# Broadcasts in attention: two chained transfers of 64 partitions instead of one of 128

## What is computed

```python
def _forward(hidden_states, wq, wk, wv, conv_q_w, conv_k_w, conv_v_w, A_log, dt_bias, ...):
    x = hidden_states
    q = short_conv(x @ wq, conv_q_w).reshape(B, T, H, DK)      # H, DK, DV = 16, 128, 128
    k = short_conv(x @ wk, conv_k_w).reshape(B, T, H, DK)
    v = short_conv(x @ wv, conv_v_w).reshape(B, T, H, DV)
    ...                                                        # feats: entropy, errors of k @ proxy_w against v
    hf = silu(silu(feats @ mlp_w1 + mlp_b1) @ mlp_w2 + mlp_b2)
    beta_fast = jax.nn.sigmoid(beta_base + beta_delta)         # and slow; lam, amp_fast, amp_slow likewise, from hf
    ...
    decay_fast = jnp.exp(g_chan[None, None] * amp_fast[..., None])
    decay_slow = jnp.exp(g_chan[None, None] * amp_slow[..., None])
    o_fast = delta_rule(qs, k_unit, v, beta_fast, decay_fast)
    o_slow = delta_rule(qs, k_unit, v, beta_slow, decay_slow)
    o = lam[..., None] * o_fast + (1.0 - lam[..., None]) * o_slow
    ...
    return o.reshape(B, T, H * DV) @ wo

def delta_rule(q, k, v, beta, decay):
    def step(S, inp):
        qt, kt, vt, bt, gt = inp
        Sd = S * gt[..., None]
        v_pred = jnp.einsum('bhk,bhkv->bhv', kt, Sd)
        S_new = Sd + jnp.einsum('bhk,bhv->bhkv', kt * bt[..., None], vt - v_pred)
        ot = jnp.einsum('bhk,bhkv->bhv', qt, S_new)
        return (S_new, ot)
```

## Time and profile before

| | us |
|---|---|
| median of 3 runs | 4295.09 |
| lowest, highest | 4289.88, 4296.61 |
| the profiled execution's own time | 4301.73 |
| its span, first to last instruction | 4299.9 |
| TensorE busy (share of the span) | 4000.7 (93%) |
| VectorE busy | 3105.3 (72%) |
| ScalarE busy | 2296.8 (53%) |
| GpSimd busy | 933.6 (22%) |
| share of 16 DMA engines in the queue of SyncE's transfers | 20.2% |

### The profile page before, as it was taken

The page is one execution under the profiler, slowest core; times in us unless marked ns, Lnnn a source line. Parts: engine busy times, 40 slices in busy tenths (PEclk is TensorE's granted clock), DMA queues, the critical chain, the costliest instruction groups (busy, mean ns, idle before and its releaser), DMA issues. The chain is left out here.

```text
span 4299.9 us, 179869 instructions
## 1 busy us (share of the span) xinstructions
PE 4000.7 (93%) x76866; PEld 2486.6 (58%) x76866; DVE 3105.3 (72%) x5135; ACT 2296.8 (53%) x6321; POOL 933.6 (22%) x1927
## 2 busy tenths in 40 slices
PE   7999999999999999999999999757879789999998
PEld 4667767767676676767667676522333334444443
DVE  4788888888888888888888887478999991212221
ACT  4577776676676667676676766444344331111110
POOL 1333333333333333333233333100000000000000
PEclk8999999999999999999999999778989899999999
DMA  2222222222221212212122221142323332000000
GB/s 76 65 60 71 65 69 68 58 76 66 63 68 59 77 52 75 70 56 78 57 70 70 63 71 49 41 148 72 94 83 96 92 121 89 29 1 30 0 20 10
DMA packets 133721, 277.31 MB, mean 64 GB/s; under 512 B 21004, under 2 KB 62496, under 8 KB 129472
## 3 DMA queue, kind: packets, MB, share of 16 engines
q1 hardware_dynamic: 132784, 265.60, 20.2%
q10 hardware_dynamic: 144, 0.20, 0.0%
HBM read 235.07 MB, written 30.67 MB: 62 GB/s over the span
## 5 line engine op out<-in xcount | busy, mean ns | idle before, releaser
L420 PE MATMUL a_pb<-a_x_t,a_w_qkv 128*128 128x512 f32 x1536 | 844.0, 641 | 15.5 <-DMA a_x_t<-in_x_t 8.2
L1318 DVE TENSOR_TENSOR a_nq<-a_nq,a_tot 128x1024 f32<-128x1024 f32 x320 | 392.8, 1227 | 133.9 <-PE a_pb L451 85.2
L1281 DVE SCALAR_TENSOR_TENSOR a_acc<-a_pb,a_taps,a_acc 128x511 f32<-128x511 f32 (+2 forms) x576 | 425.5, 739 | 31.1 <-ACT a_acc L866 17.4
L2119 PE MATMUL m_p_y<-m_h,k_ident_sb 128*128 128x512 f32 x512 | 285.4, 710 | 130.7 <-DVE m_h L2356 130.7
L2830 DVE TENSOR_TENSOR a_x_t<-f_gate,f_pb 128x512 f32<-128x512 f32 x128 | 88.0, 687 | 383.1 <-ACT f_gate L2754 383.1
L2754 ACT ACTIVATE f_gate<-f_pb 128x512 f32<-128x512 f32 x132 | 78.8, 597 | 411.7 <-PE f_pb L2695 275.4
L420 PEld LDWEIGHTS a_pb<-a_x_t,a_w_qkv 128*128 128x128 f32 x1536 | 241.1, 192 | 99.0 <-issue 67.4
L451 PEld LDWEIGHTS a_pb<-a_nq,a_ks 128*32 128x32 f32 x20480 | 214.3, 111 | 143.3 <-issue 112.8
L2350 DVE TENSOR_TENSOR_SCAN m_h<-m_da,m_h 128x2048 f32<-128x2048 f32 x64 | 283.1, 4424 | 17.7 <-ACT m_da L2262 12.4
L1718 POOL COPY a_apt<-a_apt_fine 32x256 f32<-32x256 f32 x256 | 100.5, 393 | 882.4 <-DVE a_apt_fine L1336 857.8
L2119 PEld LDWEIGHTS m_p_y<-m_h,k_ident_sb 128*128 128x128 f32 x512 | 112.7, 228 | 295.1 <-DVE m_h L2356 161.9
(11 more groups left out here) (332 smaller groups left out, 8841.6 us busy)
## 6 DMA issues: line engine op xcount, KB each, us to landing
a_rows<-rows SPq DMA_DIRECT2D x192, 512.0 KB, 3.9
a_amp_sums<-amp_sums SPq DMA_DIRECT2D x64, 508.0 KB, 3.7
attn_o<-a_o_out SPq DMA_DIRECT2D x64, 256.0 KB, 2.7
m_b_rows<-ssm_bc SPq DMA_DIRECT2D x64, 256.0 KB, 3.7
m_c_rows<-ssm_bc SPq DMA_DIRECT2D x64, 256.0 KB, 4.5
k_big<-attn_o SPq DMA_DIRECT2D x16, 1024.0 KB, 8.3
a_w_qkv<-in_w_qkv SPq DMA_DIRECT2D x48, 256.0 KB, 3.2
k_big<-in_w_gu SPq DMA_DIRECT2D x3, 1536.0 KB, 13.3
```

Source lines behind the costliest of these rows:

```text
L420: mm = nc.tensor.matmul(pb[:, V_BANK if i == P_V else KQ_BANK], w_qkv[:, i, k], x_t[:, k, b * T:(b + 1) * T], start=(k == 0), stop=(k == D ...
L1281: last = nc.vector.scalar_tensor_tensor(acc[:, i, d:T], src[:, 0:T - d], taps[:, i, 3 - d:4 - d], acc[:, i, d:T], ALU.mult, ALU.add)
L1318: last = nc.vector.tensor_tensor(part, part, spread(blocks, list(part.shape)), ALU.mult)
L2119: nc.tensor.matmul(p_y[:, et], ident[:], h[:, (b * DS + n) % 3, et], start=(n == 0), stop=(n == DS - 1), skip_group_check=True).then_inc(s ...
```

## The change

Each of the four broadcasts becomes two, of partitions 0 to 63 and of partitions 64 to 127. SyncE waits for the landing of each before it issues the next. The waits of ScalarE and VectorE now count to the second half. Nothing else is different, and no other engine's instructions move.

```diff
-                        hold(rows_in, s.due(1, 48, 0))
-                        hold(sums_in, s.due(1, 16, 0))
+                        hold(rows_in, s.due(1, 96, 0))
+                        hold(sums_in, s.due(1, 32, 0))
...
                         def rows_of(q, count):
-                            sp.dma_start(rows[:, q:q + 2].rearrange("p q t -> p (q t)"),
-                                         spread(io["rows"][r, q * TT:(q + 2) * TT].rearrange("q t -> (q t)").unsqueeze(0),
-                                                [P, 2 * T])).then_inc(rows_in, 16)
-                            hold(rows_in, s.due(1, 48, count))
+                            for part in range(2):
+                                sp.dma_start(rows[part * P // 2:(part + 1) * P // 2, q:q + 2].rearrange("p q t -> p (q t)"),
+                                             spread(io["rows"][r, q * TT:(q + 2) * TT].rearrange("q t -> (q t)").unsqueeze(0),
+                                                    [P // 2, 2 * T])).then_inc(rows_in, 16)
+                                hold(rows_in, s.due(1, 96, count + 16 * part))
 
                         rows_of(R_AMP, 16)
                         hold(tot_ready, s.due(1, 1, 0))
-                        sp.dma_start(amp_sums[:], spread(io["amp_sums"][r].unsqueeze(0), [P, PAIRS * SUMS])
-                                     ).then_inc(sums_in, 16)
-                        hold(sums_in, s.due(1, 16, 16))
-                        rows_of(R_NEG_K, 32)
-                        rows_of(R_QUERY, 48)
+                        for part in range(2):
+                            sp.dma_start(amp_sums[part * P // 2:(part + 1) * P // 2],
+                                         spread(io["amp_sums"][r].unsqueeze(0), [P // 2, PAIRS * SUMS])).then_inc(sums_in, 16)
+                            hold(sums_in, s.due(1, 32, 16 + 16 * part))
+                        rows_of(R_NEG_K, 48)
+                        rows_of(R_QUERY, 80)
...
                 def exp_e1(s):
-                    act.wait_ge(rows_in, s.due(1, 48, 16))
+                    act.wait_ge(rows_in, s.due(1, 96, 32))
...
-                    act.wait_ge(sums_in, s.due(1, 16, 16))
+                    act.wait_ge(sums_in, s.due(1, 32, 32))
...
                 def prepare_nq(s, kind):
-                    free, count, landed = ((r_sum, TT - 1, 32), (o_sum, TT, 48))[kind]
+                    free, count, landed = ((r_sum, TT - 1, 64), (o_sum, TT, 96))[kind]
                     dve.wait_ge(silued, s.due(1, 3, P_Q + 1))
-                    dve.wait_ge(rows_in, s.due(1, 48, landed))
+                    dve.wait_ge(rows_in, s.due(1, 96, landed))
```

## The result

| | before | with the change |
|---|---|---|
| median of the runs, us | 4294.58 | 4984.62 |
| lowest and highest, us | 4284.85, 4296.72 | 4969.4, 5001.07 |
| ratio, 95% interval | | 1.1613 [1.1586, 1.1641] |
| span of the profiled execution, us | 4299.9 | 4982.1 |
| mean granted clock | 0.96 | 0.90 |

The kernel is 16.1% slower, 690 us. The forecast was 4765 us (11%), the range 4570 to 5020. So the sign and the range held, and the size was a third too small: 470 us were foreseen.

A forecast was written before the change was run, and what follows sets the result against it. Each unit (one head of one batch row) was bounded by copy to first broadcast, chained broadcasts and following work: 4.7 + 25.0 + 18.2 = 47.9 us. 4301.7 + 418 + 51 (clock) = 4771, forecast 4765 us, range 4570 to 5020.

The forecast's parts named there:

- The ring: Attention, per head of one batch row: copy of rows, broadcasts, work until next copy bound its length; 39.0 of 41.37 us before.
- chain: SyncE's broadcasts of decay rates, sums, key rows, query rows, each waiting for the one before: 16.1 us, becoming 25.0.
- copy to the first broadcast: From ScalarE's `copy_rows` to SyncE's issue of the decay rates' broadcast: taken as 4.7 us.
- rest: From the reading of the query rows to the next head's copy of rows: 18.2 us, not shrinking when transfers take longer.
- rival 4: TensorE makes up the lateness behind the query rows; a gain of 2 us per unit gives 4640 us; chance 0.06.
- The room: Spare time per head of one batch row before the change, 41.37 against 39.0 us: some 2.4 us on average.
- A half's landing: Issue to landing of a lone 256 KB broadcast: 3.0 us, 0.9 less than a whole; 3.13 us from issue to issue.
- port rule: Skill page's rule for transfers into SBUF: partitions 0 to 63 reach only every second of 16 ports; given little weight.
- The clock: TensorE idles more, so its clock falls to 0.50 more often: 0.8 us per unit, 51 us in all.
- Rival 2: A half broadcast lands as slowly as a whole: 5233 us, chance 0.07; between, at 3.4 us, 4978 us, chance 0.10.
- Rival 1: A half broadcast lands as fast as a lone 256 KB load, 2.6 us: 4520 to 4580 us; chance 0.14.
- rival 3: Not slower: spare time absorbs the longer broadcasts if a half takes 2.3 us issue to issue; 4295 us; chance 0.03.

The follow-up runs named there:

- e6: Changed kernel with each half loaded from 64 separate rows of the weights `w_o` in place of a broadcast from one row: 5049.19 us, ratio 1.1719.
- e5: Changed kernel with halves of the even and the odd partitions in place of the lower and upper 64: 4855.84 us, ratio 1.1277.
- e3: Kernel before the change, with only the query rows' broadcast split into two chained halves: 4386.47 us, ratio 1.0193.
- e1: Changed kernel with both halves of a broadcast issued one behind the other and one wait per pair: 4410.46 us, ratio 1.0247.
- e8: Kernel before, four whole broadcasts issued one behind the other, sums first, no waits between, own semaphores for key and query rows: 4579.7 us, ratio 1.0629.
- e11: Kernel before, whole broadcasts in two bursts of two (decay rates and sums, then key and query rows), own semaphores: 4465.14 us, ratio 1.0368.
- e9: Kernel before, SyncE waiting only for the rows' store before the first broadcast, for the other small stores before the sums: 4312.14 us, ratio 1.0009.

## Why the prediction was right, and where it was off

**The ring: right.** In the changed kernel no slack is left between the chain and its reader, in any unit, and a unit is copy to first broadcast, chain and rest. The rest was taken as 18.2 us and measured 18.19. That is 0.4 less than the 18.59 of before, where rival 4 needed 2 us, so rival 4 falls. The copy to the first broadcast was taken as 4.7 and is 5.0; that is the mean over all units where the prediction read two.

**The room: 2.4 us taken, 1.58 measured** at the query rows (0.89 at the key rows). The remainder was in two other terms, 5.05 and 18.59 where 4.7 and 18.2 had been read. As all of them add up to the same 41.37 us, that moved little: with the chain as measured the prediction's own terms give 4.7 + 28.8 + 18.2 = 51.7 us per unit, against 52.06.

**A half's landing: mis-sized, and this is the miss.** The step "a lone broadcast of 256 KB lies between 2.6 and 3.4; I take the middle, 3.0 us" was the failing one. A half takes 3.52 us (mean), 0.12 above the upper end. From issue to issue 28.80 / 8 = 3.60 us where 3.13 was taken; eight of them are 28.8 us where 25.0 was taken, 3.8 us per unit or 243 us in all. The change's own waits of SyncE give the same (us in total, times, longest):

```profile
SPq L327 <- DMA a_rows<-rows: 1181.0, 384, 4.6
...
SPq L327 <- DMA a_amp_sums<-amp_sums: 390.8, 128, 3.6
```

(1181.0 + 390.8) / 512 + 0.45 for the issue, with 0.07 behind it as before, is 3.59 us. What failed was the choice between two neighbours: half the way from L339 to `m_b_rows`, for which no row gave a reason. Alone, a broadcast half lands in 3.5 us, where `m_b_rows` with another behind it has 3.4 at best and 3.7 as a median. That row was the only one of the same kind of access, and it was the right one, nearly unaltered. e6 shows that the broadcast isn't what makes a half of this shape slow, e5 that the choice of partitions is some of it; the rest of the distance to 2.6 is open.

**What was luck.** The branch that came true is not the one forecast: halves of 2.8 to 3.3 us had a chance of 0.60, those of 3.3 to 3.7 one of 0.10. The prediction's own sign of being wrong was a half over 3.5 us, and the mean of 3.52 stands just past it. The issues are 3.6 us apart where 3.1 was written, and the copies 52.1 where 47 to 49 was. VectorE stood some 9.2 us per unit for the key rows where 5 was written, and 2.8 for the query rows where 1 to 2 was. The time lies 35 us inside a range that is wider than the middle branch, and without the 51 us for the clock the forecast would have been 4714, 271 short.

**Which partitions: weighed too lightly.** The prediction gave the port rule little because a whole doesn't reach the ports' full rate. That is so, but e5 shows 0.31 us of a half's 3.52 for the partitions alone, and eight in a row make 2.5 us per unit.

**The clock: 51 us were added, about 24 are seen.** The granted clock did fall, from 1.00 to 0.89 in the attention stage, and stands at its lower level behind the waits, as was said. The stage, and three stretches of the unit above (columns as in rows 1):

```profile
160.00:3350.00 3190.00, 2723.91 (x70419) 1899.49 (x70418) 2150.20 (x4200) 1763.11 (x5410) 792.69 (x1831) 0.89 0.18 52
...
1385.00:1400.00 15.00, 8.62 (x121) 4.56 (x122) 5.34 (x9) 6.16 (x13) 5.80 (x11) 0.82 0.23 72
1400.00:1404.00 4.00, 4.00 (x116) 2.37 (x115) 3.62 (x6) 2.58 (x5) 0.40 (x3) 0.50 0.67 155
1404.00:1424.00 20.00, 20.00 (x558) 15.12 (x558) 18.61 (x39) 12.92 (x40) 2.37 (x9) 0.98 0.09 26
```

TensorE is busy for 8.62 of 15 us while the last halves land, and 4 us at 0.50 follow. On average the rest is 18.19 us all the same, but not in every unit alike. In the 42 units in which the granted clock of that part was above 0.98 it is 17.81 us, in the other 21 it is 18.95, and the second are the longer ones at each of the four places that a unit can have in its head (by 0.4 to 1.5 us). That makes 0.38 us per unit or 24 us in all, an estimate from units of one kernel and not from a kernel that holds the clock. In e3, where the query rows are waited for too and the clock was 0.99 in the attention stage, the rest is 18.06. So the cost is there, half of what was taken, but in a rest that is some 0.4 us shorter without it than the 18.2 read before; why it is shorter wasn't tried. Added to 18.2, the 51 us had nothing left to pay for.

**The sum with the measured terms.** 4.97 + 28.80 + 0.09 + 18.19 = 52.05 us per unit. On the profiled execution's own 4301.7 us that is 64 x 10.69 = 684, so 4986, and 4983.89 was measured. Rival 2's middle value, a half of 3.4 us, gave 4978: the right mechanism and nearly the right size, but its chain was 0.6 us short, and the clock's 51 us, too much for the ring as just said, made up for that.

**The rivals.** Rival 1 (2.6 us) is out by the landings, rival 3 with it, as is the full rival 2 (a half as long as a whole).

## What to carry to other kernels

Where transfers wait for each other, what counts is the number of landings in a row, not their bytes: half the bytes saved 0.43 of 3.95 us here, so two took 7.2 us from issue to issue where one took 4.0. A wait that the profile puts down to "issue" can often be named from what ends just before it: a landing, a step of another engine, or a packet of instructions. Look for the ring before reading busy shares: one resource at 98% and 23 us of waits hid a chain with 1.6 us of slack. Price an operation that the trace lacks by the row of the same kind of access, not by the middle between unlike rows, above all where it will be multiplied by 512.

## What the runs showed of the hardware that I had not expected

- Two halves in flight together (4.6 us) land later than one whole (3.8 us), e1.
- The same half lands in 3.21 us on every second partition and in 3.52 on the lower or the upper 64, e5 against the change.
- Four broadcasts of 512 KB at once keep the DMA engines 94% busy in the 4 us shown, and TensorE stands up to 4.5 us until 1.1 to 1.7 us behind an instruction packet; e8, and shorter in e11. The chain of waits, which looks like waste, spreads the transfers out.
- A broadcast that leaves 1.25 us earlier, beside small stores that are under way, lands only 0.2 us earlier, e9.
